# Head order, bias row, block 1's scores and one down product moved in a fused attention and FFN kernel

## What is computed

```python
xn = (x - mean) / sqrt(var + 1e-5)                      # over the features
h = tanh(xn @ W1.T + b1); s = h @ w2.T + b2             # one score per token
e = exp(s - max(s)); ctx = cumsum(e * xn) / cumsum(e)   # running mean along the sequence
attn = tanh(concat(ctx, xn) @ Wc.T + bc)
ffn = (silu(xn @ wg.T / 127) * (xn @ wu.T / 127)) @ wd.T / 127   # 768 hidden, integer weights
out = x + attn + ffn
```

## Time and profile before

| | us |
|---|---|
| three timed runs | 392.28, 393.71, 394.12 (median 393.71) |
| the profiled execution | 392.16 |
| its span, first to last instruction | 390.0 |
| busy: TensorE / VectorE / ScalarE / GpSimd | 384.7 / 291.0 / 234.7 / 214.2 |
| granted TensorE clock | 1.00 throughout |

### The profile page before, as it was taken

The page is one execution under the profiler, slowest core; times in us unless marked ns, Lnnn a source line. Parts: engine busy times, 40 slices in busy tenths (PEclk is TensorE's granted clock), DMA queues, the critical chain, the costliest instruction groups (busy, mean ns, idle before and its releaser), DMA issues.

```text
span 390.0 us, 7869 instructions
## 1 busy us (share of the span) xinstructions
PE 384.7 (99%) x2735; PEld 268.2 (69%) x2735; DVE 291.0 (75%) x604; ACT 234.7 (60%) x436; POOL 214.2 (55%) x301
## 2 busy tenths in 40 slices
PE   8999999999999999999999999999999999999996
PEld 4556676658667676766867776768677676776765
DVE  6899999969597979966679965776776766754351
ACT  4774777499977667886466575463563644536260
POOL 1468798875527999895244415765455654502000
PEclk9999999999999999999999999999999999999999
DMA  8965456565543234666300014043131340100001
GB/s 251 350 209 56 114 100 168 93 161 119 117 106 114 53 111 62 158 113 102 81 29 29 28 41 154 27 131 97 46 94 46 80 107 3 54 29 28 29 27 62
DMA packets 55775, 36.82 MB, mean 94 GB/s; under 512 B 31921, under 2 KB 51634, under 8 KB 55730
## 3 DMA queue, kind: packets, MB, share of 16 engines
q1 hardware_dynamic: 55440, 35.99, 36.8%
q10 hardware_dynamic: 290, 0.26, 0.2%
HBM read 20.45 MB, written 8.45 MB: 74 GB/s over the span
## 4 chain that ended last, share of the span: by engine, by line
PE 99%; DVE 0%; issue 0%
PE bank L783 44%; PE bank L815 43%; PE bank L835 9%; PE bank L1480 1%; PE bank L762 1%; PE bank L754 0%; PE bank L747 0%; PE bank L1487 0%; DVE sg L1507 0%; PE bank L890 0%; PE bank L896 0%; DVE xres L1219 0%; PE bank L889 0%; PE bank L883 0%; PE bank L878 0%
## 5 line engine op out<-in xcount | busy, mean ns | idle before, releaser
L815 PE MATMUL bank<-xt,narrow 128*128 128x512 f16 x768 | 177.8, 379 | 0.0
L815 PEld LDWEIGHTS bank<-xt,narrow 128*128 128x128 f16 x768 | 75.2, 98 | 74.8
L783 PE MATMUL bank<-narrow,wide 128*128 128x256 f16 x792 | 96.4, 273 | 0.0
L783 PE MATMUL bank<-narrow,xt 128*128 128x256 f16 x744 | 89.9, 273 | 0.0
L1355 POOL TENSOR_TENSOR wide<-ex,wide 128x512 f16<-128x512 f32 x32 | 41.1, 1303 | 86.6 <-ACT wide L997 86.6
L976 ACT ACTIVATE sg<-bank 128x512 f32<-128x512 f32 x96 | 57.0, 597 | 52.1 <-PE bank L815 50.1
L1210 DVE SCALAR_TENSOR_TENSOR bank<-bank,sg 128x512 f32<-128x512 f32 x96 | 66.2, 694 | 26.9 <-PE bank L815 22.7
L783 PEld LDWEIGHTS bank<-narrow,xt 128*128 128x128 f16 x744 | 72.8, 98 | 18.0
L783 PEld LDWEIGHTS bank<-narrow,wide 128*128 128x128 f16 x792 | 77.5, 98 | 9.4
L983 ACT ACTIVATE wide<-bank 128x512 f16<-128x512 f32 x90 | 53.3, 595 | 42.5 <-DVE bank L1210 40.1
L1215 DVE TENSOR_TENSOR wide<-bank,wide 128x512 f16<-128x512 f32 x90 | 60.4, 677 | 12.6 <-ACT wide L983 11.5
(11 more groups left out here) (111 smaller groups left out, 264.6 us busy)
## 6 DMA issues: line engine op xcount, KB each, us to landing
rows<-scratch SPq DMA_DIRECT2D x16, 512.0 KB, 5.0
out_y<-xres SPq DMA_DIRECT2D x31, 256.0 KB, 2.1
xres<-in_x SPq DMA_DIRECT2D x15, 512.0 KB, 5.5
xt<-xt SPq DMA_TRANSPOSE x56, 2.5
wide<-in_wg SPq DMA_DIRECT2D x2, 384.0 KB, 5.9
wide<-in_wu SPq DMA_DIRECT2D x2, 384.0 KB, 7.4
wide<-in_wd SPq DMA_DIRECT2D x1, 768.0 KB, 8.9
wide<-in_wc SPq DMA_DIRECT2D x1, 512.0 KB, 9.9
```

The source lines that it names most:

```text
L783: return pe.matmul(dst, lhs, rhs, start=False, stop=stop, skip_group_check=True)
L815: mm = pe.matmul(b[:, :], pg.up(which, k, j), pg.xn(sx, k, tok), start=n == 0, stop=n == len(todo) - 1)
```

## The change

Six edits. WARM goes from 9 to 7 and FILL from 4 to 7. The bias row is issued between tiles 2 and 3 of x on ScalarE's queue. In the planner, block 1's two score parts get places 4.3 and 5.0 instead of 3.1 and 3.5 (its transposes Lb stay), and the down product of block 3, part 1, goes from 25.91 to 27.51, past the hidden parts 26 and 27 and the first softmax transpose M1 (26.4). The first seed of block 0 no longer needs W1's high half; that half needs the first seed instead, so ScalarE does seed, W1h, seed. Tile 3's transposes leave the planner's list and are issued inside first_scores, behind the two products of tile 0; the planner still counts them at their old place.

```diff
-WARM, FILL = 9, 4
+WARM, FILL = 7, 7
...
-        place += [(after + 0.9 + 0.01 * pr, ("D", i, pr)) for pr in shares(i)]
+        place += [(after + (2.5 if (i, pr) == (BLK_SEQ // 2 - 1, 1) else 0.9) + 0.01 * pr, ("D", i, pr)) for pr in shares(i)]
...
-        place += [(turn + 1.1, ("S", i, 0)), (turn + 1.5, ("S", i, 1))]
+        score = turn + (2.3 if i == 1 else 1.1)
+        place += [(score, ("S", i, 0)), (score + (0.7 if i == 1 else 0.4), ("S", i, 1))]
...
     if kind == "W1h":
-        return []
+        return [] if wide else [(("Ss", 0, 0), 0)]
...
     if kind == "Ss" and i == 0:
-        return [(("W1h", 0, 0), 0)]
+        return [(("W1h", 0, 0), 0)] if x else []
...
                     onto(t, 0, 0)
+                    if t == 0:
+                        open_bank(pe, fits, "L0", 0, 3)
+                        turn_tile(pe, 3)
...
-            elif kind == "L0":
+            elif kind == "L0" and n < 3:
...
             load_first(act, 2)
+            act.dma_start(b_row, biases[0:D].rearrange("(o d) -> o d", o=1)).then_inc(s_b, 16)
             load_first(act, 3)
-            act.dma_start(b_row, biases[0:D].rearrange("(o d) -> o d", o=1)).then_inc(s_b, 16)
```

## The result

The changed kernel took 395.06 us (median of 10 runs, 394.36 to 395.31), the kernel before 392.51 in the same comparison (10 runs, 391.73 to 394.16). The ratio is 1.0057, 95% interval 1.0041 to 1.0072: slower by 0.57%. The forecast was no change within 0.5% (84%), so the direction was wrong, though 395.06 lies inside the range. The sum of the parts was +0.60; measured are +2.5 between the medians. Three executions far outside all others (450 and 1449 us of the kernel before, 1053 us of b_row) are left out of every count.

What follows compares the result with a forecast made beforehand. TensorE's unbroken stream of products was taken to bound the kernel. Terms of +0.37 (a) and +0.23 (d), the rest 0, gave +0.60 on 393.0, the middle of four times of before: 393.6 us, range 392.1 to 395.4.

Steps and rivals of the forecast that it cites:

- What bounds the kernel: Whole span: TensorE's unbroken stream is the bound, so order can win only losses ahead of it or in the tail, 0.35 us.
- (a): Head loads: bias row sent ahead of tile 3 delays tile 3's statistic by 0.37 us; bounds 0 and 1.17.
- (b): Head, nine warm-ups to seven and four fillers to seven: cost 0, hidden behind (a) by 0.1 us.
- Rival 1: Fillers: the clock rises later, only after them, and transposes run at double pitch; +2.5 us, 395.5; 10%.
- (c): Head, ScalarE: first seed ahead of W1's high half; cost 0, gain 0.
- (d): Head: tile 3 turned behind tile 0's two products leaves TensorE idle before tile 3's first product; +0.23 us, bounds -0.35 and +0.5.
- (e): Block 1's scores later: a swap among products with ready inputs; cost 0, upper bound 1.3 us if a bank or seed is late.
- Rival 2: At (f) or (e): the planner's new order leaves a TensorE break; up to 3.2 us, 396.2; 7%.
- I am wrong if a break stands behind 10 us: Sign on TensorE: after the head its stream should have no break; one behind 10 us would refute the prediction.
- (f): Down product (3, 1) moved behind the softmax's first transpose: cost 0, upper bound its own 2.62 us.
- (g): Tail of the kernel: nothing edited, cost 0.
- Rivals 3 and 4: Head: old spread came from the bias row, 392.8, 13%; new head order pays, at most -0.35, 392.6, 10%.

Runs made afterwards that it cites:

- b_row: The kernel before with only the bias row issued between tiles 2 and 3 of x; median 394.02 us, ratio 1.0028.
- b_seed_turn: The kernel before with only the first seed ahead of W1's high half and tile 3 turned behind tile 0's products; median 394.02 us, ratio 1.0029.
- run 16: Not a follow-up run: "run" is a verb here, in "two reductions, which run 16 and 21 us behind their scores on VectorE".
- b_down: The kernel before with only down product (3, 1) placed later; groups at 391.74 and 393.65 us, ratio 1.0008.

## Why the prediction was wrong, step by step

- **What bounds the kernel**: right. Inside the span no time changed that wasn't a loss ahead of the stream or a break in it. The 2.16 us outside it, taken as fixed, were not: they became 1.8.
- **(a), the step that failed first.** "I take 0.37, the row's issue time on tile 3's own latency": it was 1.10 in the profile after and 1.33 to 1.76 in four others (statistic at 5.74 to 6.17 instead of 4.41), near the upper bound of 1.17 and beyond it. The latency was not tile 3's own; it was that of a transfer with no rival on the other queue. The Trainium skill ("DMA: Bandwidth & Descriptors", Issuing engines are not separate DMA queues) had it that loads issued by different engines interleave on the same DMA engines; the runs agree, with 3.7 and 4.3 us to landing beside W1 and 2.8 with nothing beside it. With the bound of 1.17 the sum would have been 0.8 higher. The value was taken from the wrong row: tile 3's own 3.0 us at its old place, instead of the 3.9 of W1, whose issue falls within 0.1 us of tile 3's new one (b_row measured 3.9). That an idle TensorE may also lose its clock was not in the sum.
- **(b), cost 0**: right where the clock rises early. Rival 1 is what the profiled execution shows: fillers slow to 8.76 (predicted 8.49; the passes took 1.15 instead of 0.85 to the next start) and six transposes at double pitch. It had 10%, and it costs nothing against an execution of before whose rise was as late. The mistake was in how the four times of before were read: they were seen to lie in two groups and averaged to 393.0, a value no run takes.
- **(c), cost 0**: right; ScalarE was idle ahead of the conversions.
- **(d), +0.23**: right in mechanism and size where the clock rises early (+0.2 in b_seed_turn; +0.4 in its upper group).
- **(e), cost 0**: the second step that failed. The bound of 1.3 held 1.01, but the mechanism given for it (a bank or a seed late) was not the one. "A swap among products all of whose inputs lie ready" looked at TensorE alone; the due times of two reductions, which run 16 and 21 us behind their scores on VectorE (35.68 and 43.42 against 19.58 and 22.62), are computed from the same place. Rival 2 (a break from the planner's new order at (e) or (f), 7%) is what happened at (e); its reason against (eight banks, and TensorE products between that need neither) looked at TensorE alone too. "I am wrong if a break stands behind 10 us" was the sign, and it stood at 45. The description of the kernel says that a changed place may change the order on all engines behind it; the prediction followed that on TensorE and not on VectorE, which was busy 11.86 of 12 us there in the kernel before:

```profile
34.00:46.00 12.00, 12.00 (x75) 7.13 (x73) 11.86 (x42) 7.75 (x15) 9.34 (x28) 1.00 0.67 109
```

- **(f), cost 0**: right for TensorE's stream; outside the span it took 0.3 off the time, which nothing in the prediction foresaw. **(g), cost 0**: right, no trace shows a change.
- **Sum**: +0.60 was made of 0.37 and 0.23. Measured terms with an early clock are 1.1 to 1.7, 0.2 and 1.0, less 0.3, so 2.0 to 2.6 in all. That 395.06 lies inside the range is luck: the top of the range was set by rival 1, a late clock on the middle of 393.0, not by a larger (a) or a break at (e). Rivals 3 and 4 did not happen; the spread of before was the clock's, not the row's landing.

What remains open: whether seven warm-ups ahead of one-row passes raise the share of late rises (17 of 24 against 26 of 48); why that share differs so much among kernels with the same head (9 of 12 for b_down, 9 of 35 for before beside it); why the clock rises late in some executions only if the passes run over one row; and what the later down product shortens outside the span.

## What to carry to other kernels

A transfer that is moved later by half a microsecond may land more than a microsecond later: price it by what is in flight on all queues at its new place, not by its old latency. When a planner moves a step, list every step whose due time is computed from it, on each engine, and look at how busy that engine is there and what GpSimd does beside a VectorE instruction with two SBUF inputs. When the times of a kernel fall into two groups, find what tells the groups apart before adding to their middle: a loss may be hidden in one and full in the other.

## Not expected

Two VectorE instructions became 0.85 and 0.94 us longer, from 0.39 and 0.42 to 1.24 and 1.36, with no change in their work, for running 5 us later, beside GpSimd's subtractions. A row of 1 KB ahead of a tile cost the tile 0.2 us with an empty other queue and 1.1 to 1.8 with a full one. And two passes over one row of the array, at the lower clock, take 1.22 us where two over 128 rows take 1.06, for the same number of columns. Last, moving one down product late in the first sequence took 0.3 us off the time outside the profiled span.
